# Graph network, output stage: eight result buffers and one power instruction for two pairs of tiles

## The reference, cut to what matters

```python
x = _linear_diffusion(x, src, dst)      # six steps, in the stage before
x = x @ W_out.T + b_out
...
x = _layernorm(x + _L3_gnn_ref(x, ...), axis=-1)   # (y - mean) / sqrt(var + 1e-5)
```

## Time and profile before

| | |
|---|---|
| time, median of 3 runs | 3975.6 us (3973.98 to 3982.41) |
| time of the profiled execution | 3978.42 us |
| its span | 3976.6 us |
| mean granted TensorE clock | 0.919 |
| output stage, first load issued to last write issued | 3768.4 to 3966.3 us |
| instructions | 57087 |

### The profile page before, as it was taken

How to read it: one execution, slowest core, us unless ns; L and a number is a source line. 1 busy time by engine, 2 the same in 40 slices (tenths; PEclk the granted TensorE clock), 3 DMA queues, 4 the chain that set the end, 5 groups by cost and what they waited for, 6 DMA issues and landing times. The chain is left out here.

```text
span 3976.6 us, 57087 instructions
## 1 busy us (share of the span) xinstructions
PE 3270.6 (82%) x14868; PEld 2599.0 (65%) x14868; DVE 2815.4 (71%) x7915; ACT 1892.1 (48%) x5401; POOL 2282.9 (57%) x2529
## 2 busy tenths in 40 slices
PE   5999926687675998469999972999999999999775
PEld 4888725575464665237777761878878787878654
DVE  5767668697784666875666651888888888888633
ACT  3777615576232111233333330566656665666455
POOL 4766500587475664133333321878788787878577
PEclk8999959899898999559999995999999999999898
DMA  4887739443574332463333329767767676767654
GB/s 144 245 247 242 225 113 367 128 131 109 153 218 128 93 88 60 140 200 96 114 113 113 111 87 323 228 200 234 227 205 235 201 233 199 233 198 233 188 189 156
DMA packets 690470, 710.73 MB, mean 179 GB/s; under 512 B 73444, under 2 KB 644190, under 8 KB 689796
## 3 DMA queue, kind: packets, MB, share of 16 engines
q1 hardware_dynamic: 592204, 484.13, 39.3%
q0 software_dynamic: 68288, 181.26, 16.1%
q10 hardware_dynamic: 29660, 41.70, 3.1%
HBM read 427.77 MB, written 296.22 MB: 182 GB/s over the span
## 5 line engine op out<-in xcount | busy, mean ns | idle before, releaser
L595 POOL DMA_INDIRECT s_i_messages<-h,table_row x600 | 645.6, 1076 | 192.2 <-issue 81.5
L2610 PE MATMUL s_i_bank<-s_i_messages,s_i_equal 128*128 128x256 f32 x1200 | 363.5, 386 | 78.0 <-DMA s_i_messages<-h,table_row 74.1
L776 PE MATMUL s_n_bank<-w,n_xt 128*128 128x256 f32 x1280 | 308.1, 384 | 21.4 <-DMA n_xt<-in_x_t 21.4
L2647 DVE SCALAR_TENSOR_TENSOR s_i_y<-s_i_bank,s_i_scale,s_i_acc 128x256 f32<-128x256 f32 x600 | 284.5, 475 | 44.1 <-PE s_i_bank L2610 24.5
L794 PE MATMUL s_n_bank<-w_out,n_ht 128*128 128x256 f32 x1280 | 309.9, 386 | 0.9 <-ACT n_ht L804 0.9
L785 PE MATMUL s_n_bank<-n_x3t,w_in 128*128 128x256 f32 x1280 | 304.1, 381 | 0.0
L816 ACT ACTIVATE n_w<-n_w,n_small 128x256 f32<-128x256 f32 x320 | 145.1, 500 | 308.1 <-POOL n_small L843 307.4
L2610 PEld LDWEIGHTS s_i_bank<-s_i_messages,s_i_equal 128*128 128x128 f32 x1200 | 218.6, 193 | 108.5 <-issue 79.5
L776 PEld LDWEIGHTS s_n_bank<-w,n_xt 128*128 128x128 f32 x1280 | 247.2, 193 | 56.7 <-DMA n_xt<-in_x_t 21.8
L794 PEld LDWEIGHTS s_n_bank<-w_out,n_ht 128*128 128x128 f32 x1280 | 247.6, 194 | 36.0 <-ACT n_ht L804 1.3
L785 PEld LDWEIGHTS s_n_bank<-n_x3t,w_in 128*128 128x128 f32 x1280 | 244.3, 191 | 33.9 <-ACT n_x3t L674 0.2
(11 more groups left out here) (426 smaller groups left out, 9401.6 us busy)
## 6 DMA issues: line engine op xcount, KB each, us to landing
h<-s_i_y SPq DMA_DIRECT2D x600, 128.0 KB, 3.2
n_xt<-in_x_t SPq DMA_DIRECT2D x160, 256.0 KB
out<-n_w SPq DMA_DIRECT2D x160, 256.0 KB, 2.2
s_i_equal<-eq_tab SPq DMA_DIRECT2D x600, 64.0 KB
x<-s_x_rows SPq DMA_DIRECT2D x100, 256.0 KB
out<-s_a_hs SPq DMA_DIRECT2D x100, 128.0 KB
proj_dst<-s_a_hd SPq DMA_DIRECT2D x100, 128.0 KB
h<-s_h_rows SPq DMA_DIRECT2D x50, 256.0 KB, 4.0
```

The lines of the kernel that those rows point to most:

```text
L595: return net.nc.gpsimd.indirect_dma_start(out, None, table, bass.IndirectOffsetOnAxis(index, 0))
L776: mm = self.nc.tensor.matmul(self.pr[:, g * self.D:(g + 1) * self.D], self.XT[u][:, c, g * P:(g + 1) * P], self.net.w12[:, c, :], start=c ...
L2610: nc.tensor.matmul(banks[r % 4][:, 0:D], EQ[q % NM][:], M[q % NM][:], start=True, stop=True).then_inc(summed, 1)
L2647: V.scalar_tensor_tensor(Y[q % NY][:], banks[r % 4][:, 0:D], scale[:, s, t:t + 1], acc[:, t, :], ALU.mult, ALU.add).then_inc(added, 1)
```

## The change

`Y` gets eight buffers and eight `written` semaphores. One `variance` and one `power` now serve two units m: units 2m and 2m+1. They run in odd turns, on four columns instead of two, `variance` after the square of unit 2m+1. The norm and the write of a unit come one turn later (i-4 instead of i-3), and there is one more turn. `S` has 12 columns, `junk` holds four tiles. The square's wait is now on the variance instead of the power. POOL has one more wait ahead of the power, on the norms of the units that used the same columns.

```diff
-    G, NB = 2, 4
+    G, NB, NY = 2, 4, 8
...
-        Y = st.sb("j_y", [P, G, D], n=4)
-        junk = st.sb("j_junk", [P, G, D])
-        S = st.sb("j_small", [P, 8], n=2)
+        Y = st.sb("j_y", [P, G, D], n=NY)
+        junk = st.sb("j_junk", [P, 2 * G, D])
+        S = st.sb("j_small", [P, 6 * G], n=2)
...
-        TURNS = U + 4
+        TURNS = U + 5
...
-            def power(k):
-                if 0 <= k < U:
-                    gp.wait_ge(var, k + 1)
-                    nc.gpsimd.tensor_tensor(S[k % 2][:, 4:4 + G], S[k % 2][:, 2:2 + G], net.neg_half[:, 0:G], ALU.pow).then_inc(dev, 1)
+            def power(m):
+                if 0 <= m < U // 2:
+                    gp.wait_ge(var, m + 1)
+                    past(gp, o_ready, 2 * m - 2)
+                    nc.gpsimd.tensor_tensor(S[m % 2][:, 4 * G:6 * G], S[m % 2][:, 2 * G:4 * G], net.neg_half[:, 0:2 * G], ALU.pow).then_inc(dev, 1)
...
-            for i in range(TURNS):
-                power(i - 2)
-                write(i - 3)
+            for i in range(TURNS):
+                if i % 2:
+                    power((i - 3) // 2)
+                write(i - 4)
...
             def square(k):
                 if 0 <= k < U:
                     act.wait_ge(y_ready, k + 1)
-                    past(act, dev, k - 1)
+                    past(act, var, k // 2 - 1)
...
             def norm(k):
                 if 0 <= k < U:
-                    act.wait_ge(dev, k + 1)
+                    act.wait_ge(dev, k // 2 + 1)
...
-                norm(i - 3)
+                norm(i - 4)
                 square(i - 2)
...
-                    past(dve, written[k % 4], 16 * G * (k // 4))
+                    past(dve, written[k % NY], 16 * G * (k // NY))
...
-            def variance(k):
-                if 0 <= k < U:
-                    dve.wait_ge(squared, k + 1)
-                    past(dve, o_ready, k - 1)
-                    V.tensor_scalar(S[k % 2][:, 2:2 + G], S[k % 2][:, 0:G], EPS, None, ALU.add).then_inc(var, 1)
+            def variance(m):
+                if 0 <= m < U // 2:
+                    dve.wait_ge(squared, 2 * m + 2)
+                    past(dve, dev, m - 1)
+                    V.tensor_scalar(S[m % 2][:, 2 * G:4 * G], S[m % 2][:, 0:2 * G], EPS, None, ALU.add).then_inc(var, 1)
             for i in range(TURNS):
                 bias(i)
                 join(i - 1)
-                variance(i - 2)
+                if i % 2:
+                    variance((i - 3) // 2)
```

More of the change, by code:

```diff
@@ L2670, in output @@
         XT = st.sb("j_xt", [P, C, G * P], n=2)
-        Y = st.sb("j_y", [P, G, D], n=4)
-        junk = st.sb("j_junk", [P, G, D])
-        S = st.sb("j_small", [P, 8], n=2)
+        Y = st.sb("j_y", [P, G, D], n=NY)
+        junk = st.sb("j_junk", [P, 2 * G, D])
+        S = st.sb("j_small", [P, 6 * G], n=2)
         a_in, x_in = (st.sem(f"j_{n}", NB) for n in ("acc_loaded", "x_loaded"))
-        written = st.sem("j_written", 4)
+        written = st.sem("j_written", NY)
         b_ready, tp_made, xt_ready, projected, y_ready, squared, var, dev, o_ready = (st.sem(f"j_{n}") for n in (
@@ L2678, in output @@
         tps, prs = (st.ps(f"j_ps_{n}", 2) for n in ("t", "p"))
-        TURNS = U + 4
+        TURNS = U + 5
+        assert U % 2 == 0
         past = Unmet.past
@@ L2706, in write @@
                     for g in range(G):
-                        nc.gpsimd.indirect_dma_start(a["out"], bass.IndirectOffsetOnAxis(net.end_node[:, k * G + g:k * G + g + 1], 0), Y[k % 4][:, g, :], None,
-                                                     bounds_check=N - 1, oob_is_err=False).then_inc(written[k % 4], 16)
+                        nc.gpsimd.indirect_dma_start(a["out"], bass.IndirectOffsetOnAxis(net.end_node[:, k * G + g:k * G + g + 1], 0), Y[k % NY][:, g, :], None,
+                                                     bounds_check=N - 1, oob_is_err=False).then_inc(written[k % NY], 16)
             for i in range(TURNS):
-                power(i - 2)
-                write(i - 3)
-            for u in range(4):
-                gp.wait_ge(written[u], 16 * G * len(range(u, U, 4)))
+                if i % 2:
+                    power((i - 3) // 2)
+                write(i - 4)
+            for u in range(NY):
+                gp.wait_ge(written[u], 16 * G * len(range(u, U, NY)))
         @block.tensor
@@ L2748, in square @@
                     act.wait_ge(y_ready, k + 1)
-                    past(act, dev, k - 1)
+                    past(act, var, k // 2 - 1)
                     for g in range(G):
-                        sq = nc.scalar.activation(junk[:, g, :], Y[k % 4][:, g, :], ACT.Square, scale=D ** -0.5, accum_out=S[k % 2][:, g:g + 1])
+                        at = k % 2 * G + g
+                        sq = nc.scalar.activation(junk[:, at, :], Y[k % NY][:, g, :], ACT.Square, scale=D ** -0.5, accum_out=S[k // 2 % 2][:, at:at + 1])
                     sq.then_inc(squared, 1)
@@ L2755, in norm @@
                 if 0 <= k < U:
-                    act.wait_ge(dev, k + 1)
+                    act.wait_ge(dev, k // 2 + 1)
                     for g in range(G):
-                        nm = nc.scalar.activation(Y[k % 4][:, g, :], Y[k % 4][:, g, :], ACT.Copy, scale=S[k % 2][:, 4 + g:5 + g])
+                        at = (4 + k % 2) * G + g
+                        nm = nc.scalar.activation(Y[k % NY][:, g, :], Y[k % NY][:, g, :], ACT.Copy, scale=S[k // 2 % 2][:, at:at + 1])
                     nm.then_inc(o_ready, 1)
@@ L2777, in join @@
                     dve.wait_ge(b_ready, k + 1)
-                    past(dve, written[k % 4], 16 * G * (k // 4))
-                    V.tensor_tensor(Y[k % 4][:], two(prs[k % 2]), X[k % NB][:], ALU.add).then_inc(y_ready, 1)
-            def variance(k):
-                if 0 <= k < U:
-                    dve.wait_ge(squared, k + 1)
-                    past(dve, o_ready, k - 1)
-                    V.tensor_scalar(S[k % 2][:, 2:2 + G], S[k % 2][:, 0:G], EPS, None, ALU.add).then_inc(var, 1)
+                    past(dve, written[k % NY], 16 * G * (k // NY))
+                    V.tensor_tensor(Y[k % NY][:], two(prs[k % 2]), X[k % NB][:], ALU.add).then_inc(y_ready, 1)
+            def variance(m):
[3 more added lines that the diff above has]
+                    V.tensor_scalar(S[m % 2][:, 2 * G:4 * G], S[m % 2][:, 0:2 * G], EPS, None, ALU.add).then_inc(var, 1)
             for i in range(TURNS):
```

## The result

The changed kernel takes 3966.26 us (median of 7 runs, 3960.53 to 3968.34) against 3975.42 for the one before (7 runs): ratio 0.9975, 95% interval 0.9965 to 0.9985. That is 9.2 us faster. The forecast was 3947, the range 3941 to 3962: the sign was right, the size was three times too large. Measured twice more, on two other chips, the ratio was 0.9967 (0.9954 to 0.9980) and 0.9966 (0.9953 to 0.9979); the medians there are 12.1 and 14.5 us apart.

The account below looks back on a forecast made before the run. POOL was taken to bound the output stage: 181.0 us from first to last write, less 18.6 (powers) and 12.2 (waits), plus 1.5 and 0.7, gives 152.4. The gain of 28.6 us put the median at 3947, range 3941 to 3962.

Parts of the forecast that it names:

- POOL bounds the stage and its list gives the time: Output stage: POOL hardly pauses, so shortening its list shortens the stage; 181.0 us from first to last write.
- my sum: Output stage, first to last write on POOL: 181.0 - (18.6 + 12.2) + 1.5 + 0.7 = 152.4 us.
- filling and small waits: Output stage: 1.5 us lost once in filling, 0.7 us for POOL's additional wait and the wider `variance`.
- The eight buffers end the join's waits for landings: Output stage: a buffer is held 21.1 us against 24.2 available, so 12.2 us of POOL idleness go.
- The new pair on POOL, 6.05 us, made of undisturbed durations: POOL, output stage: one power and four DMAs, 1.00 + 2.51 + 2.54 = 6.05 us, 3.03 per unit.
- The power at 1.00, 0.1 us ahead of the second addition: POOL beside DVE: power starts after one bias, 0.1 us before the other, and stays at 1.00 us.
- the rival that I gave 0.18: The power meets the bias addition in each pair: 11.7 us given back, time 3959; chance 0.18.
- my bound: POOL, output stage: upper bound of the four-column power if its order with the bias turns, 1.51 us.
- The chain on ACT, 3.88 us: From a power's end to the next `variance`, 3.88 us; 0.9 us of slack before POOL arrives.
- Filling: Start of output stage: first write moves from 3785.3 to 3785.5, second power delayed; 1.5 us lost once.
- The base of the sum: Output stage of the profiled execution before: 181.0 us first to last write, 12.2 of them POOL waiting for `variance`.
- DMA engines and the clock: Two rivals: DMA limit at 221 GB/s, 3960, chance 0.10; TensorE's lower clock, 4020, chance 0.05 with another slower ring.

Follow-up runs that it names:

- the paired order: Changed kernel with b_out added in place in PSUM before the join: first to last write 152.2 us, ratio 0.9925 against the kernel before.
- one half: Kernel before with eight result buffers and eight semaphores, still one power per unit: 3959.3 us, ratio 0.9954, stage 178.2 us.
- the other half: Powers paired on top of eight buffers, which is the changed kernel: stage 181.8 to 182.5 us against 178.2 with the buffers only.

## Why the prediction failed, by its own steps

- *POOL bounds the stage and its list gives the time*: right. With nothing in its way the paired order took 152.2 us from first to last write; my sum had 152.4. Part of that match is luck: the powers took 1.3 us more than in the sum, and the 2.2 us that it allowed for filling and small waits were hardly used.
- *The eight buffers end the join's waits for landings*: right, and needed (9.37 us a pair with four).
- *The new pair on POOL, 6.05 us, made of undisturbed durations*: this is the step that failed. It measured 6.72. I had laid the two bias additions beside the power alone, and not beside the DMAs, whose slowing I put at nothing. In my own schedule the first addition starts at 3.96 and the fourth DMA at 4.08 us after the last power; it takes 0.39 us more. Over the 22 slow DMAs that is 8.1 us. In the output stage of before no DMA was slow, but its earlier stages, from which I took the slow powers, showed this too. Two lines of the trace of before:

```profile
3574.39 0.69 DVE L690 TENSOR_TENSOR n_z<-n_z,beta_bc 128x512 f32<-128x512 f32 x1
3574.56 1.36 POOL L595 DMA_INDIRECT s_i_messages<-h,table_row  x1 [0.30 <-PE s_i_bank L2610]
```

In that trace 154 indirect DMAs start 0.05 to 0.17 us after a 128x512 operation of DVE with both inputs in SBUF (L688 or L690), and all take 1.36 to 1.51 us; the median of that line's largest group is 0.95. The cost could have been read there before the forecast.
- *The power at 1.00, 0.1 us ahead of the second addition*: the rival that I gave 0.18 happened, though by another way than the one I had in mind: without the slow DMA the power would have started 0.04 us ahead of the addition; pushed behind the addition's start, it took 1.24, not the 1.51 of my bound. Undisturbed it takes 1.05, not 1.00. The two cost 3.8 and 1.3 us.
- *The chain on ACT, 3.88 us*: 3.85 (3854.47 to 3858.32), right, and its slack held.
- *Filling*: the first write came 1.0 us later than before, counted from the first load, and not 0.2, but POOL did not stop before the second power. On balance as forecast.
- *The base of the sum*: it took 12.2 us of POOL's waiting from one execution. A second one had 5.1, and its stretch from first to last write was 176.2 us, not 181.0, so part of what I meant to win was not there in every run. The stage gained 16.2 us against one profile and 11.1 against the other; the medians say 9, 12 and 15. In the first sitting the difference is plain sums: 16.2, less the 4.1 by which the changed profile's stage began later, less the 3.0 by which the profiled execution of before lay above its median, is 9.1.
- *DMA engines and the clock*: no part of it. In the changed kernel the stretch 3900 to 3920 moved 234 GB/s at a share of 0.75, above the 221 of the earlier trace rows that the rival took as a limit. PE's clock made no second bound: POOL went on at 6.5 to 6.7 us a pair where the granted clock was 0.86.

The forecast missed by 19 us. Of these, 11.5 are the stretch from first to last write (163.9 against 152.4), which the two collisions fill; 1 is the later first write; 4.1 the later start of the stage, which is chance; and 2.8 the step from the profiled execution down to the median, for the changed kernel's profiled execution was itself the median. The collisions alone would have left the time at 3959, inside the range. It fell outside by 4 us because the rest came on top; the range's upper end, 3962, was made of single mishaps.

## To carry to other kernels

When an edit shifts the order of two engines that meet in SBUF, lay the new schedule of one against all instructions of the other, not only against the one that was seen to suffer, and ask where each start will fall; here an addition 0.17 us ahead of a DMA and one 0.35 us ahead of a power cost 12 us. Look for such pairs in all stages of the trace at hand, not only in the one that is changed. Before pricing a wait that depends on landings, look at a second execution. And try the parts of an edit alone: here, by the stage's time, one half made the whole gain and the other half took a little of it back, until an operand was moved to PSUM.

## What the runs showed of the hardware

An indirect DMA issued by POOL is held up by a DVE addition with both inputs in SBUF that starts 0.17 us before it: 1.36 instead of 0.97 us, ending 0.84 after the addition. One that starts 0.31 us into the DMA costs it nothing (0.97), and takes its own usual 0.68 us. An addition with one operand in PSUM that starts 0.13 to 0.24 us before the DMA costs nothing either (0.97 to 1.04, 22 cases), nor does one 0.05 us before the power (1.05). The Trainium skill (SBUF — State Buffer, "Who interferes with whom") says that an addition with both inputs in SBUF contends with GpSimd's reads and infers that descriptor writing is not held up; the runs show the indirect DMA, taken whole, being held up, and do not show whether by a read of its offsets. A power on 128x4 takes 1.05 us against 0.74 on 128x2, so four columns cost 0.43 us less than twice two.
